# The causal masks of the last attention as products of 32 rows in the scores' own tiles

## The reference, cut to what matters

```python
Q, K, V = split_heads(x @ W_q.T), split_heads(x @ W_k.T), split_heads(x @ W_v.T)   # 16 heads of 8
Q, K = _rope(Q, pos), _rope(K, pos)
score = jnp.einsum('bnqd,bnkd->bnqk', Q, K) / jnp.sqrt(jnp.float32(D_K))
causal = jnp.triu(jnp.ones((s, s), dtype=bool), k=1)
score = jnp.where(causal[None, None], -jnp.inf, score)
attn = jax.nn.softmax(score, axis=-1)
out = jnp.einsum('bnqk,bnkd->bnqd', attn, V)
x = x + (out.transpose(0, 2, 1, 3).reshape(b, s, D_MODEL) @ W_o.T)
```

## Time and profile before

| | |
|---|---|
| median of 3 runs | 1343.97 us (1343.85 to 1346.62) |
| the profiled execution | 1353.68 us |
| its span, first to last instruction | 1351.9 us |
| PE busy | 1222.1 us, 90% |
| DVE busy | 830.8 us, 61% |
| ACT busy | 653.7 us, 48% |
| POOL busy | 285.1 us, 21% |
| mean granted clock of TensorE | 0.979 of full speed |

### The profile page before, as it was taken

The page is one execution under the profiler, slowest core; times in us unless marked ns, Lnnn a source line. Parts: engine busy times, 40 slices in busy tenths (PEclk is TensorE's granted clock), DMA queues, the critical chain, the costliest instruction groups (busy, mean ns, idle before and its releaser), DMA issues.

```text
span 1351.9 us, 27707 instructions
## 1 busy us (share of the span) xinstructions
PE 1222.1 (90%) x10063; PEld 960.2 (71%) x10063; DVE 830.8 (61%) x1781; ACT 653.7 (48%) x1338; POOL 285.1 (21%) x381
## 2 busy tenths in 40 slices
PE   5999971889999899999999999889999999989999
PEld 2555620458788889887887888478889866657777
DVE  4888678564555566657777565456564477764242
ACT  2666686445434334444454444233434457755553
POOL 4877300120003142330000014043340021200000
PEclk9999995999999999999999999999999999999999
DMA  9000010501142113103106101032102000000000
GB/s 326 2 1 2 11 69 0 210 1 63 35 177 84 56 53 102 49 27 147 67 1 249 68 7 48 24 101 67 47 18 87 1 2 2 3 2 1 1 16 16
DMA packets 42898, 75.86 MB, mean 56 GB/s; under 512 B 3848, under 2 KB 33680, under 8 KB 41872
## 3 DMA queue, kind: packets, MB, share of 16 engines
q1 hardware_dynamic: 38672, 65.69, 13.4%
q0 software_dynamic: 4096, 8.40, 2.1%
HBM read 59.78 MB, written 14.29 MB: 55 GB/s over the span
## 4 chain that ended last, share of the span: by engine, by line
PE 76%; DVE 13%; ACT 5%; issue 3%; DVEq 1%; DMA 1%; POOL 0%; ACTq 0%; SPq 0%; POOLq 0%
PE bank L1869 7%; PE bank L1880 7%; PE bank L1865 7%; PE bank L1924 5%; PE bank L1611 4%; PE bank L1856 4%; PE bank L1934 3%; PE bank L1616 3%; PE bank L1618 3%; PE bank L1617 3%; PE bank L1681 2%; PE bank L1849 2%; PE bank L1851 2%; PE bank L1850 2%; PE bank L1697 2%
## 5 line engine op out<-in xcount | busy, mean ns | idle before, releaser
L2127 ACT ACTIVATE SC<-bank 128x512 f32<-128x512 f32 x192 | 114.3, 595 | 223.1 <-PE bank L1865 124.0
L2214 DVE SCALAR_TENSOR_TENSOR SC<-bank,SM,SC 128x512 f32<-128x512 f32 x128 | 95.8, 748 | 123.2 <-PE bank L1869 102.5
L1880 PE MATMUL bank<-A,SC 128*128 x1024 | 137.0, 277 | 7.9 <-DVE SC L2214 7.1
L1869 PE MATMUL bank<-X,SC 128*128 128x128 f32 x1024 | 136.8, 277 | 4.4 <-DVE SC L2489 3.9
L1865 PEld LDWEIGHTS bank<-X,SC 128*128 128x128 f32 x1024 | 126.1, 192 | 20.0 <-issue 13.0
L1865 PE MATMUL bank<-X,SC 128*128 128x128 f32 x1024 | 136.1, 276 | 3.7 <-ACT SC L2111 2.5
L1880 PEld LDWEIGHTS bank<-A,SC 128*128 128x128 f32 x1024 | 125.4, 192 | 17.4 <-issue 16.5
L1869 PEld LDWEIGHTS bank<-X,SC 128*128 128x128 f32 x1024 | 124.5, 192 | 6.9 <-DVE SC L2489 6.7
L1924 PE MATMUL bank<-A 128*128 128x128 f32 x736 | 100.4, 280 | 16.0 <-DVE A L2639 10.5
L1924 PEld LDWEIGHTS bank<-A 128*128 128x128 f32 x736 | 90.1, 193 | 21.1 <-ACT A L2152 13.0
L2790 POOL TENSOR_SCALAR A<-A,CC 128x256 f32<-128x256 f32 (+1 forms) x128 | 55.4, 451 | 189.7 <-DVE A L2306 102.2
(11 more groups left out here) (340 smaller groups left out, 2530.7 us busy)
## 6 DMA issues: line engine op xcount, KB each, us to landing
A<-in_moe SPq DMA_DIRECT2D x36, 768.0 KB, 10.5
A<-xs SPq DMA_DIRECT2D x20, 256.0 KB, 3.7
ys<-A SPq DMA_DIRECT2D x20, 256.0 KB, 2.3
BW<-in_l1f SPq DMA_DIRECT2D x2, 2048.0 KB, 7.3
BW<-in_l2f SPq DMA_DIRECT2D x1, 3456.0 KB, 10.7
BW<-in_l1c SPq DMA_DIRECT2D x1, 3072.0 KB, 16.7
BW<-in_l3f SPq DMA_DIRECT2D x1, 2816.0 KB, 9.8
A<-in_l1c SPq DMA_DIRECT2D x1, 2560.0 KB, 8.7
```

Source lines behind the costliest of these rows:

```text
L1869: m = e.matmul(at["pu"].ap[:, cut(q)], wx[:, cut(4 + q)], x, start=True, stop=True)
L1880: m = e.matmul(o, at["h"].ap[:, cut(q)], W[:, bass.ds(r + (1024 + 128 * q), 128)], start=k == 0 and q == 0, stop=k == 1 and q == 3)
L2127: e.activation(at["h"].ap, at["pg"].ap, ACT.Gelu_apprx_tanh).then_inc(at["gelu"][0], 1)
L2214: return e.scalar_tensor_tensor(out=o, in0=a, scalar=s, in1=b, op0=o1, op1=o2)
```

## The change

The block `tri` goes out of `CONST`; `MKB` becomes 128 columns wide. For a row group, `IDB` now holds in its first 64 columns the 32x32 identity and 32 zero columns, in its second 64 columns zeros and the identity. `MKB` holds in its first 64 columns the triangle of 32 rows and 32 columns of -3e38, in its second 64 columns 32 zero columns and the triangle. They are made on DVE by three memsets and 16 copies of 32x32. In `scores` both banks are waited for first; then come two rounds (`part`) of four bf16 products, one for each g, in the tiles of 32 rows by 64 columns that the scores use: eight products of 256 columns per unit in place of two. The scores behind them are the same.

```diff
@@ CONST
-CONST = [("ident", 128), ("hm4", 4), ("mask", 128), ("tri", 64), ("sumw", 128), ...
+CONST = [("ident", 128), ("hm4", 4), ("mask", 128), ("sumw", 128), ...
@@ build
-        MKB = sb("MKB", 64, BF16)[:, :]
-        IDB = sb("IDB", 128, BF16)[:, :]
+        MKB, IDB = sb("MKB", 128, BF16)[:, :], sb("IDB", 128, BF16)[:, :]
@@ tensor, scores
-                    for x in range(2):
-                        over(at["pa"][x])
-                        e.matmul(pa[x][:, :, keys - 64:keys], IDB, bc_mid(MKB, 4), start=True, stop=False)
+                    over(at["pa"][0])
+                    over(at["pa"][1])
+                    for part in (slice(0, 64), slice(64, 128)):
+                        for g in range(4):
+                            rows, to = slice(32 * g, 32 * g + 32), slice(64 * (g // 2), 64 * (g // 2) + 64)
+                            e.matmul(pa[g % 2][to, :, keys - 64:keys], IDB[rows, part], bc_mid(MKB[rows, part], 4),
+                                     start=part.start == 0, stop=False)
@@ vector, top_max
-                    e.tensor_copy(IDB, ident)
-                    e.tensor_copy(MKB, c("tri")).then_inc(t_idb[0], 1)
+                    e.memset(IDB[:, 32:96], 0.0)
+                    e.memset(MKB[:, 32:64], -3e38)
+                    e.memset(MKB[:, 64:96], 0.0)
+                    for g in range(4):
+                        for a in (0, 96):
+                            rows, block = slice(32 * g, 32 * g + 32), slice(32 * g, 32 * g + 32)
+                            e.tensor_copy(IDB[rows, a:a + 32], ident[rows, block])
+                            i = e.tensor_copy(MKB[rows, a:a + 32], c("mask")[rows, block])
+                    i.then_inc(t_idb[0], 1)
```

More of the change, by code:

```diff
@@ L88, in layout_of @@
     return out, at
-CONST = [("ident", 128), ("hm4", 4), ("mask", 128), ("tri", 64), ("sumw", 128), ("sumw2", 64), ("condT", 16),
+CONST = [("ident", 128), ("hm4", 4), ("mask", 128), ("sumw", 128), ("sumw2", 64), ("condT", 16),
          ("As0", 128), ("Bs0", 128), ("Wb0", 128), ("bb0", 1), ("cond", 128), ("ph", 130), ("am", 130),
@@ L2878 @@
     vals = {
-        "ident": np.eye(128, dtype=f), "trig": trig, "mask": mask, "hm4": hm4, "sumw": sumw, "sumw2": sumw2, "tri": np.concatenate([mask[0:64, 0:64]] * 2, 0), "ctab": ctab, "stab": stab,
+        "ident": np.eye(128, dtype=f), "trig": trig, "mask": mask, "hm4": hm4, "sumw": sumw, "sumw2": sumw2, "ctab": ctab, "stab": stab,
         "iota": rows(np.arange(8, dtype=f)), "cond": rows(cond), "condT": np.repeat(cond.T, 16, axis=0),
```

## The result

| | before | after |
|---|---|---|
| median of 9 runs each | 1345.19 us | 1350.22 us |
| ratio | | 1.0032, 95% interval 1.0022 to 1.0043 |
| the profiled execution | 1353.68 us | 1345.86 us |
| its span | 1351.9 us | 1344.0 us |

The change makes the kernel slower, by 4.3 us by the ratio. In two later comparisons the same kernel stood at 1.0043 and 1.0037. The forecast was 1346.2 (1341.8 to 1350.6), +2.25 us: the sign is right and the range holds the median, but the rise is about twice the forecast, and 0.56 had gone to "within 0.2%". Of the 4.0 us between forecast and median 1.2 belong to the kernel before, whose median of nine runs lies that much above the 1343.97 that the forecast started from.

What follows compares the result with a forecast made beforehand. PE was taken to bound the kernel, with DVE and POOL also tight in the first attention. PE saving -2.6, DVE delay +4.95, smaller transfer -0.1 gave +2.25 on 1343.97: 1346.2 us, range 1341.8 to 1350.6.

Steps and rivals of the forecast that it cites:

- The saving on PE: Last attention: new mask rounds save 0.128 us in 19 units and 0.02 in seven others, 2.6 us in all.
- The two places that were to give time back: Last attention: waits at the second mask for ACT L2027, where PE's saving is given back, three units each.
- rival (d): Nothing given back at the two waits, short loads, copies passing freely: -2.8 us, 1341.2 us; chance 0.09.
- Rival (c): Last attention: bf16 tiles get in each other's way, a round takes 0.216 us; +7.8 us, 1351.8 us; chance 0.07.
- The open load of the first round: Last attention: unhidden weight load of a unit's first mask round, taken as 0.027 us, between 0.011 and 0.05.
- The copies: First attention: 16 DVE copies wait for seams between POOL instructions, so L2321 starts at 128.96, 5.15 us late.
- I take two: First attention: two copies pass at each POOL seam, so 16 need eight seams, the last at 127.86.
- (a): First attention: three copies pass per POOL seam, 1343.9 us, or all pass freely, 1342.5; chance 0.36 for both forms.
- (b): First attention: one copy passes per POOL seam; +6.4 us, 1350.4 us; chance 0.10.
- everything behind follows PE. Nothing else covers it.: Behind PE's late scores in the first attention: no gap makes the delay good; 4.95 us reaches PE and stays.
- DVE's term: First attention: the late L2321 delays PE's scores through ACT's L2027, adding 4.95 us.
- The start: Transfer of constants that begins the chain: 32 KB less of `c1`, at most 0.25 us, taken as 0.1 us saved.

Runs made afterwards that it cites:

- experiment 1: The changed kernel with its three memsets and 16 copies moved on DVE to behind the first attention; 1349.95 us against 1350.98 before, ratio 1.0000.
- experiment 5: The changed kernel with memsets at the head of DVE's list and the 16 copies on ACT at the start; ratio 0.9967 to the kernel before, 0.9983 when repeated.

## Why the prediction was right or wrong

**The saving on PE: right.** From first mask to second round of scores the unit takes 0.46 us, as forecast. Over the stage, from the first mask to the first mask of the last unit, 2.2 us were saved (101.41 to 99.25), where the sum had 2.6. Two units in a row took 5.28 us for 5.50, which is 0.11 us a unit and not 0.128. The two places that were to give time back did: from the last transpose to the mask product that waits it is 0.78 and 0.64 us, where it was 0.43. The bound of 3.9 us in rival (d) doesn't follow from the terms beside it, which give 3.6 at most (23 units at 0.144, nine at 0.036). Rival (c) falls: the four bf16 tiles of a round start 3 to 4 ns apart, and a round takes 0.109 us, not 0.216, with two row tiles writing different halves of the partitions of one bank side by side. That four tiles take the time of one product holds in both types: one bf16 product of 256 columns took 0.109 us, and one fp32 product of 512 columns, as the trace records it, 0.429 (L1773 of the kernel before, starts at 1098.57 and 1099.00), 0.215 for 256, against 0.216 for an fp32 round and 0.109 for a bf16 one. The open load of the first round was 0.134 - 0.109 = 0.025 us, where the sum had its estimate of 0.027.

**The copies: mechanism right, size off.** "I take two" per seam: it was one to three. L2331 came 4.2 us late, not 5.15, between the forecast and (a) with its three per seam; its place is 127.73, the forecast had 128.96. One per seam, (b), is excluded, and that its 1350.4 us lies nearest to the measured time is chance. The copies of 1.00 and 1.25 us, which start 0.08 and 0.06 us behind the recorded start of a product and of an addition, lay still until those were through; others that start 0.05 to 0.07 us behind the recorded start of one of POOL's instructions passed. What decides between them, no run here shows.

**The step that failed: "everything behind follows PE. Nothing else covers it."** The sum stopped at PE's first late scores. It let 4.95 us through, and there 4.1 arrived (3.83 and the 0.27 by which all was early; 4.1 and 5.1 in two other executions, counted the same way). Then came 1.9 us more (2.7 and 3.2), so DVE's term was 6.0 us where 4.95 stood (6.8 and 8.3). Two things make it: PE's wait of 4 us is followed by the half clock, which is most of it in the changed kernel, and the late DVE meets POOL a second time. The shift puts the small SBUF instructions of `top_mix`, untouched by the change, from POOL's short instructions beside its long ones. The rows that would have told it were at hand: the earlier trace rows is one of the five, held by POOL. That the range holds the time all the same is partly luck: 0.85 us too much at the scores stands against 1.9 us that the sum hadn't.

**The start: small.** The transfer of the constants takes 6.39 us in the chain, for 6.70: 0.3 us rather than 0.1. This rests on one execution of the kernel before: its first product behind the transfer (L1639) starts at 11.16 us, those of the thirteen traces with the smaller block at 10.65 to 11.17.

**The sum** by the profile of after is -2.2 + 6.0 - 0.3 = +3.5 us, and with DVE's term in the two other executions, 6.8 and 8.3, +4.3 and +5.8. The ratios of the three comparisons give 4.3, 5.8 and 5.0, so the sum fits them only to within 1.5 us. The growth is shown to need one of two causes (table above); what the half clock costs in the median of many executions stays open, since the run without it came out even with the changed kernel, to within some 2 us either way. Rival (d) falls.

The better version follows from the same reading: nothing in the masks is slow, only the place of the copies. On ACT at the start they cost nothing that shows, and the kernel gains 0.2 to 0.3%.

## What to carry to other kernels

Small set-up work costs what its place makes it cost: 16 copies and three memsets were 1.9 us on DVE alone and 4.75 us beside POOL; with the copies on ACT at the start nothing of them shows. When a delay is passed on through a stage in which small instructions of one engine lie still beside the other's (copies of 0.16 us for up to 1.25 here), don't stop the sum at the first late instruction: look up which small instructions of the next 15 us are moved from beside short instructions of the other engine to beside long ones. A wait like the 4 to 5 us here is to be priced with the half clock behind it (0.50 for 3.4 to 6.8 us here), but check whether another engine isn't just as late by then, for two such costs in parallel count once.

## What the hardware showed beyond that

- Four bf16 products in 32x64 tiles, two to a PSUM bank in different halves of the partitions, run as one: 3 to 4 ns apart, 256 columns in 0.109 us.
- Copies of 32x32 follow each other on DVE every 0.09 us when POOL is at rest, with 0.18 us at each fourth (experiment 1); on ACT every 0.12 us, with 0.22 us at each fourth (experiment 5).
- Behind PE's wait of 4.03 us the granted clock was 0.66 over the 5 us from 130 us on, that is 0.50 for some two thirds of them; in the kernels in which PE idled 1.39, 1.44 or 1.96 us it stayed at 1.00. In other executions of the changed kernel the low level held for about twice as long (0.57 and 0.74, 0.50 and 0.85, in two stretches of 5 us).
- Small DVE instructions with SBUF operands, not only casts, are held by POOL: five that take 1.1 us beside short POOL instructions took 3.0 to 3.6 beside long ones.
